# Position tables of a phasor stage made through PSUM, its first loads in another order, its last output tiles begun with two units open

## The reference, cut

```python
k_real = (x @ Wk).reshape(B, T, H, D)
v = (x @ Wv).reshape(B, T, H, D)
k = exp(1j * (k_real * 10.0))
rotors = exp(1j * (t[:, None, None] * freqs))
mem = cumsum(v * rotors);        out_pos = real(mem * conj(rotors)) / sqrt(t + 1)
ks = roll(k, 1), ks[0] = 0
mem = cumsum(v * conj(ks));      out_assoc = real(mem * k) / sqrt(t + 1)
out = out_pos * g_pos + out_assoc * g_assoc
y = out @ Wo
```

## Time and profile before

| | us |
|---|---|
| median of 3 runs | 3190.17 |
| lowest, highest | 3188.63, 3192.77 |
| the profiled execution | 3188.64 |
| its span | 3186.8 |
| mean granted TensorE clock | 0.961 of full speed |
| stage a, up to the first load of the next stage | 953.5 |

### The profile page before, as it was taken

The page is one execution under the profiler, slowest core; times in us unless marked ns, Lnnn a source line. Parts: engine busy times, 40 slices in busy tenths (PEclk is TensorE's granted clock), DMA queues, the critical chain, the costliest instruction groups (busy, mean ns, idle before and its releaser), DMA issues. The chain is left out here.

```text
span 3186.8 us, 38521 instructions
## 1 busy us (share of the span) xinstructions
PE 2836.8 (89%) x12161; PEld 1226.6 (38%) x12161; DVE 1842.2 (58%) x2419; ACT 2018.3 (63%) x2642; POOL 1304.6 (41%) x795
## 2 busy tenths in 40 slices
PE   1799999999988999655999999999999999969998
PEld 0355555555553444331323232323333332234443
DVE  7899999999974453454354444444534442044444
ACT  4554555455434555424979797888878888935554
POOL 7699898889872220051313132222213230021210
PEclk8899999999998999867999999999999999989999
DMA  2000011001003220205463553545462717231112
GB/s 79 0 30 27 23 39 33 26 20 39 20 24 110 67 66 29 88 14 109 51 133 54 103 85 78 92 85 93 72 115 47 126 27 146 27 113 42 64 53 66
DMA packets 164017, 200.46 MB, mean 63 GB/s; under 512 B 16504, under 2 KB 118272, under 8 KB 163840
## 3 DMA queue, kind: packets, MB, share of 16 engines
q1 hardware_dynamic: 163840, 198.25, 28.2%
HBM read 139.49 MB, written 58.72 MB: 62 GB/s over the span
## 5 line engine op out<-in xcount | busy, mean ns | idle before, releaser
L1819 ACT ACTIVATE b_pr<-b_ps 128x1024 f32<-128x1024 f32 x1024 | 1003.0, 1025 | 256.0 <-PE b_ps L1916 251.6
L1916 PE MATMUL b_ps<-b_st 128*128 128x512 bf16 x2048 | 591.8, 386 | 71.1 <-DMA b_st<-b_scratch 33.9
L1898 PE MATMUL b_acc<-b_pr,b_vaug 128*32 128x512 f32 x4096 | 548.6, 608 | 0.4 <-ACT b_pr L1819 0.4
L1916 PEld LDWEIGHTS b_ps<-b_st 128*128 128x128 bf16 x2048 | 150.5, 98 | 649.2 <-ACT b_pr L1819 380.3
L1217 PE MATMUL f_po<-f_s,f_w 128*128 128x512 f32 x768 | 352.0, 600 | 10.1 <-DVE f_xr L1002 6.3
L990 DVE TENSOR_TENSOR f_turned<-f_cs,f_s 128x1024 f32<-128x1024 f32 x96 | 119.4, 1244 | 364.7 <-ACT f_cs L1119 359.7
L604 PE MATMUL a_pv<-a_xnT,a_wv 128*128 128x512 f32 x512 | 249.9, 612 | 48.2 <-DVE a_mem L389 31.4
L596 PE MATMUL a_pu<-a_xnT,a_wk 128*128 128x512 f32 x512 | 237.4, 607 | 36.2 <-DVE a_frac L350 30.3
L1083 ACT ACTIVATE f_h<-f_po,f_b 128x512 f32<-128x512 f32 x192 | 131.9, 687 | 215.8 <-PE f_po L1217 215.8
L1535 POOL TENSOR_TENSOR b_SQ<-b_A 128x1024 f32<-128x1024 f32 x32 | 64.7, 2022 | 466.9 <-DVE b_A L1632 466.9
L643 PE MATMUL a_py<-a_wo,a_out 128*128 128x256 f32 x960 | 228.3, 381 | 0.0
(11 more groups left out here) (247 smaller groups left out, 4659.2 us busy)
## 6 DMA issues: line engine op xcount, KB each, us to landing
b_st<-b_scratch SPq DMA_DIRECT2D x512, 128.0 KB, 6.9
b_scratch<-b_parts SPq DMA_DIRECT2D x32, 768.0 KB, 8.2
f_xl<-x SPq DMA_DIRECT2D x16, 1024.0 KB, 5.5
f_xr<-x SPq DMA_DIRECT2D x16, 1024.0 KB, 6.8
a_xl<-in_L_attn_a_x_dram SPq DMA_DIRECT2D x16, 512.0 KB, 4.3
x<-a_xr SPq DMA_DIRECT2D x32, 256.0 KB, 2.2
x<-f_xr SPq DMA_DIRECT2D x8, 1024.0 KB, 4.5
b_xl<-x SPq DMA_DIRECT2D x8, 1024.0 KB, 7.7
```

The source lines that it names most:

```text
L1819: nc.scalar.activation(pr[:, 4 * (blk % 2) + j, :], ps[:, j % 2, :], ACT.Exp, scale=SC).then_inc(S["probs_done"], 1)
L1898: x = nc.tensor.matmul(acc[32 * j:32 * j + 32, h * 512:(h + 1) * 512], vaug[:, kt, c:c + 32], pr[:, 4 * (kt % 2) + j, h * 512:(h + 1) * 51 ...
L1916: x = nc.tensor.matmul(ps[:, j % 2, h * 512:(h + 1) * 512], st[:, g % 2, 1, j, kt * P:(kt + 1) * P], st[:, g % 2, 0, j, h * 512:(h + 1) * ...
```

## The change

The order of loads: x of batch 0 comes before wk, wk gets a semaphore of its own. The whole turns k of `reduce` and the second step of the wrap are kept in po, a PSUM tensor of stage a that nothing uses during the start, so that an operation of VectorE there has one tensor in SBUF. The first step of the wrap is made by ScalarE (`turns`, an Identity with scale and bias), the second and the addition by VectorE (`wrap`), the clamp by GpSimd. GpSimd makes all eight angles first, with the means between, and scales wk. The powers come later and read a tile of their own (tpos). `front(0)` stands after table 4 and `fraction(0)` after wrap(5). At the end four tiles are begun with c = 4 and 5 only, then four more, then c = 6 for all, then c = 7 for all; the last two additions of unit 63 are VectorE's.

```diff
@@ sync
                 sp.dma_start(freq_rows[:], ...).then_inc(freq_loaded, 16)
-                sp.dma_start(wk_sb[:], ...).then_inc(w_loaded, 16)
+                for h in range(2):
+                    sp.dma_start(xl[:, h * NJ:(h + 1) * NJ, :], xi[0, h]).then_inc(xl_loaded, 16)
+                sp.dma_start(wk_sb[:], ...).then_inc(wk_loaded, 16)
                 for a in range(HPT):
                     sp.dma_start(gates[...], ...).then_inc(w_loaded, 16)
-                for h in range(2):
-                    sp.dma_start(xl[:, h * NJ:(h + 1) * NJ, :], xi[0, h]).then_inc(xl_loaded, 16)
@@ gpsimd
-                post(NC * b + c, c, free)
+                post(NC * b + c, c, free, last and c == NC - 1)
-                def wrap(c):
-                    k = cos_t[:, c, :]
-                    pool.wait_ge(reduced, c + 1)
-                    nc.gpsimd.tensor_scalar(k, sin_t[:, c, :], 1.0 / TWO_PI, MAGIC, ALU.mult, ALU.add).then_inc(wrap_done, 1)
-                    pool.wait_ge(wrap_done, 2 * c + 1)
-                    nc.gpsimd.tensor_scalar(k, k, -MAGIC, -TWO_PI, ALU.add, ALU.mult).then_inc(wrap_done, 1)
+                def clamp(c):
+                    th = sin_t[:, c, :]
+                    pool.wait_ge(wrapped, c + 1)
+                    nc.gpsimd.tensor_scalar(th, th, PI_LOW, -PI_LOW, ALU.min, ALU.max).then_inc(clamped, 1)
-                for c in range(3):
+                for c in range(4):
                     angle(c)
+                means(0)
+                for c in range(4, NC):
+                    angle(c)
+                pool.wait_ge(wk_loaded, 16)
+                nc.gpsimd.tensor_scalar(wk_sb[:], wk_sb[:], TURN, 0.0, ALU.mult, ALU.add).then_inc(wk_scaled, 1)
+                scales(0)
+                for c in range(2):
+                    clamp(c)
                 ...
-                means(0)
-                for c in range(NC):
-                    wrap(c)
+                for c in range(2, NC):
+                    clamp(c)
                     if c == 3:
                         ...
-                    if c + 3 < NC:
-                        angle(c + 3)
-                    if c == 0:
-                        scales(0)
@@ vector
+                turns = po[:].rearrange("p a n -> p (a n)")
                 def reduce(c):
-                    th, k = sin_t[:, c, :], cos_t[:, c, :]
+                    th, k = sin_t[:, c, :], turns
                     dve.wait_ge(angle_done, c + 1)
+                    if c == 1:
+                        dve.wait_ge(reduced, 1)
+                    if c >= 2:
+                        dve.wait_ge(wrapped, c - 1)
                     ...
-                def clamp(c):
+                def wrap(c):
                     th = sin_t[:, c, :]
-                    dve.wait_ge(wrap_done, 2 * c + 2)
-                    nc.vector.tensor_tensor(th, th, cos_t[:, c, :], ALU.add).then_inc(wrapped, 1)
-                    dve.wait_ge(wrapped, c + 1)
-                    nc.vector.tensor_scalar(th, th, PI_LOW, -PI_LOW, ALU.min, ALU.max).then_inc(clamped, 1)
+                    dve.wait_ge(turns_done, c + 1)
+                    ...
+                    nc.vector.tensor_scalar(turns, cos_t[:, c, :], MAGIC, -TWO_PI, ALU.subtract, ALU.mult).then_inc(wrap_done, 1)
+                    dve.wait_ge(wrap_done, c + 1)
+                    nc.vector.tensor_tensor(th, th, turns, ALU.add).then_inc(wrapped, 1)
                 for c in range(NC):
                     reduce(c)
-                    if c == 1:
-                        dve.wait_ge(w_loaded, N_W)
-                        nc.vector.tensor_scalar(wk_sb[:], wk_sb[:], TURN, None, ALU.mult).then_inc(wk_scaled, 1)
                     if c >= 1:
-                        clamp(c - 1)
-                    if c == NC - 1:
+                        wrap(c - 1)
+                    if c == NC - 2:
                         fraction(0)
-                clamp(NC - 1)
+                wrap(NC - 1)
                 ...
                 batch(B - 1, last=True)
+                nc.vector.tensor_tensor(o, o, turn_c[:], ALU.add).then_inc(added, 1)
+                ...
+                nc.vector.tensor_tensor(o, o, turn_v[:], ALU.add).then_inc(unit_done, 1)
@@ scalar
+                def turns(c):
+                    act.wait_ge(reduced, c + 1)
+                    nc.scalar.activation(cos_t[:, c, :], sin_t[:, c, :], ACT.Identity, bias=cst[:, 0:1], scale=1.0 / TWO_PI).then_inc(turns_done, 1)
                 token_sums(0)
+                turns(0)
                 token_vars(0)
+                turns(1)
                 normalise(0, range(NT))
                 transposed(0)
                 for c in range(NC):
+                    if c + 2 < NC:
+                        turns(c + 2)
                     act.wait_ge(clamped, c + 1)
                     ...
-                    if c == NC - 3:
+                    if c == NC - 4:
                         front(0, 0, first=True)
@@ tensor
+                def begin(t):
+                    nc.tensor.matmul(tail[t], diag[:, t, :], xr[:, t, :], start=True, stop=False)
+                    for c in range(HC, NC - 2):
+                        nc.tensor.matmul(tail[t], out[:, c, t * P:(t + 1) * P], wo_sb[:, c, :], start=False, stop=False)
-                pe.wait_ge(unit_done, NC * B - 1)
+                pe.wait_ge(unit_done, NC * B - 2)
                 pe.wait_ge(xt_done, 4 * B)
                 pe.wait_ge(frac_done, NC * B)
                 pe.wait_ge(wo_done, 2 * NG * (B - 1) + NG)
+                for t in range(4):
+                    begin(t)
                 pe.wait_ge(odd_done, 2 * NC * B)
                 pe.wait_ge(even_done, 2 * NC * B)
-                for t in range(NT):
+                for t in range(4, NT):
                     if t == NT - 2:
                         pe.wait_ge(last_turned, NC * B)
-                    ...
+                    begin(t)
+                pe.wait_ge(unit_done, NC * B - 1)
+                for t in range(NT):
+                    nc.tensor.matmul(tail[t], out[:, NC - 2, ...], wo_sb[:, NC - 2, :], start=False, stop=False)
                 pe.wait_ge(unit_done, NC * B)
```

More of the change, by code:

```diff
@@ L93, in phase_a @@
         gates = s.sb("gates", [P, NC, 2])
-        sm = s.sb("sm", [P, 9, NT])
+        sm = s.sb("sm", [P, 10, NT])
         cst = s.sb("cst", [P, 4])
@@ L116, in phase_a @@
         w_loaded = s.sem("w_loaded")
+        wk_loaded = s.sem("wk_loaded")
         freq_loaded = s.sem("freq_loaded")
@@ L125, in phase_a @@
         reduced = s.sem("reduced")
+        turns_done = s.sem("turns_done")
         wrapped = s.sem("wrapped")
@@ L163, in phase_a @@
         xsum, vsum, ve, rstd, nmean = (sm[:, i, :] for i in range(5))
-        tcol, root, iroot, nmr = (sm[:, i, :] for i in range(5, 9))
-        N_W = 16 * (3 + HPT)
+        tcol, root, iroot, nmr, tpos = (sm[:, i, :] for i in range(5, 10))
+        N_W = 16 * (2 + HPT)
         N_SA = 3 * NC
@@ L186, in _ @@
                 sp.dma_start(freq_rows[:], freqs.rearrange("(c a) d -> c (a d)", a=HPT)).then_inc(freq_loaded, 16)
-                sp.dma_start(wk_sb[:], wk.rearrange("(k p) n -> p k n", p=P)).then_inc(w_loaded, 16)
+                for h in range(2):
+                    sp.dma_start(xl[:, h * NJ:(h + 1) * NJ, :], xi[0, h]).then_inc(xl_loaded, 16)
+                sp.dma_start(wk_sb[:], wk.rearrange("(k p) n -> p k n", p=P)).then_inc(wk_loaded, 16)
                 gv = gate.rearrange("(c a) g -> a c g", a=HPT)
@@ L261, in scales, with post @@
                     nc.gpsimd.tensor_tensor(nmr, nmean, rstd, ALU.mult).then_inc(rstd_done, 1)
-                def post(n, c, free):
+                def post(n, c, free, end=False):
                     s, o = c % 2, out[:, c, :]
@@ L275, in post @@
                     nc.gpsimd.tensor_tensor(halves(o), pair_of(s, 2), of_tokens(cos_k[:, s, :]), ALU.mult).then_inc(turned, 1)
+                    if end:
+                        return
                     pool.wait_ge(added, 2 * n + 1)
@@ L340, in _ @@
                 nc.vector.tensor_copy(turn_c[:], rnd[:].bitcast(I32)).then_inc(setup_v, 1)
-                nc.vector.tensor_copy(ve, tcol.bitcast(I32)).then_inc(setup_v, 1)
+                nc.vector.tensor_copy(tpos, tcol.bitcast(I32)).then_inc(setup_v, 1)
                 dve.wait_ge(freq_psum, 1)
@@ L362, in reduce @@
                     nc.vector.scalar_tensor_tensor(th, k, C2 / C1, th, ALU.mult, ALU.add).then_inc(reduced, 1)
-                def clamp(c):
+                def wrap(c):
                     th = sin_t[:, c, :]
-                    dve.wait_ge(wrap_done, 2 * c + 2)
-                    nc.vector.tensor_tensor(th, th, cos_t[:, c, :], ALU.add).then_inc(wrapped, 1)
-                    dve.wait_ge(wrapped, c + 1)
-                    nc.vector.tensor_scalar(th, th, PI_LOW, -PI_LOW, ALU.min, ALU.max).then_inc(clamped, 1)
+                    dve.wait_ge(turns_done, c + 1)
+                    if c + 1 < NC:
```

(41 more changed lines are left out.)

5 lines of the change are left out of this document (3 added, 2 removed).

## The result

The changed kernel took 3171.44 us (median of 5, 3165.83 to 3174.11) against 3189.89 for the kernel before: ratio 0.9941, 95% interval [0.993, 0.9953], 18.5 us less. The forecast was 3170.4 (3162 to 3178). One later run of the changed kernel took 3819.82 us at a mean granted TensorE clock of 0.727 and is in none of the times given here.

A forecast was written before the change was run, and what follows sets the result against it. VectorE was taken to bound the start of stage a and TensorE its end. Start 13.7 us plus end 6.1 gave 19.8 us off the median 3190.17: 3170.4 us, range 3162 to 3178.

The forecast's parts named there:

- Unit 0 at 69.0: Start of stage a: VectorE begins its first unit at 69.0 us instead of 81.07, 12.1 us earlier.
- the pitch: Start-to-start time of VectorE's table operations with PSUM: 1.255 us taken, between 1.22 and 1.32, six operations a table.
- The new wait before the first fraction: VectorE waits 2.8 us, since front(0) is behind turns(6) and table 4 on ScalarE.
- x and the scales: Start of stage a: sums start near 6.5 us instead of 18.74; GpSimd's scales end at 19.7 instead of 31.08.
- The slack at turns(2): ScalarE finishes turns(2) at 29.3 us, VectorE wants it at 29.9: 0.6 us to spare.
- GpSimd's first unit: GpSimd, which waits for all tables until 88.74 us, has them at 74.5; the first scan ends at 74.8.
- The end: TensorE's output tiles closing stage a start 3.5 us earlier, the clock stays at 1.00, finishing at 943.8: 6.1 us gained.
- The additions on VectorE: End of stage a: moving the last two additions from GpSimd to VectorE is worth nothing.
- What carries the start: VectorE's tables cost 7.5 us each, no less than 7.2; the gain is waits (15.7 us) and scaling (1.5) that go.
- the forecast's premise: Start of stage a: VectorE and GpSimd hold each other up in SBUF; VectorE's PSUM operands leave GpSimd free, 1.13 us per operation.
- The surcharge of a PSUM source: VectorE's table operations: the skill's 62 extra cycles per read, 2 us in all, would make 3172.4; the forecast took none.
- The rival of a fast tensor_scalar with PSUM: VectorE's table tensor_scalars run at twice the element rate, 0.76 us pitch: gain 27 us, 3163; chance 0.04.

The follow-up runs named there:

- the filled kernel: The kernel before with 13 identity matmuls into an unused PSUM tile, ahead of TensorE's wait for unit 62's output; 3195.55 us, ratio 1.0015.

## Why the prediction was right

The sum said 19.8 us in the profiled execution's terms; stage a gave 18.7, the span 17.2, the medians 18.5. That the median came within 1.1 us of the forecast, and stage a too, is in part luck. The kernel before came out 0.3 us lower than the median that the forecast started from. And the wait of VectorE at the odd product had its short value, 17.1 us, in both profiled executions: the second profile of the changed kernel has 18.7 there, and by it stage a is only 16.6 us shorter.

- *Unit 0 at 69.0*: it was 70.13. The term that was mis-sized is the pitch. I took 1.255 us from one row's gap of 0.04 us; the durations were right (1.22 to 1.23), but at two of the six operations, after the fourth and the sixth, the gap is 0.11, and the mean pitch is 7.70 / 6 = 1.283. Over 46 operations that is 1.3 us, more than the whole miss.
- *The new wait before the first fraction*, 2.8 us forecast: 2.70.
- *x and the scales*: sums at 6.44 (6.5), normalising at 18.79 (19.7), as GpSimd was even less held up than I allowed. The slack at turns(2) was 2.0 us and not 0.6.
- *GpSimd's first unit* at 74.8: 76.19, with unit 0; the 1.61 us before the second fraction went as forecast. Start in all 12.56 us (928.32 - 915.76, the last odd product) against 13.7.
- *The end*, 6.1 us: 6.14 (25.19 - 19.05). Its two parts are shown apart: 2.6 us of clock, in the filled kernel and in the tiles themselves (20.1 us of TensorE before, 17.5 after), and 3.5 us of earlier start (from 1.54 us behind the start of the last odd product to 1.98 ahead of it). The additions on VectorE were put at nothing, and are nothing.
- *What carries the start.* The prediction said that VectorE's own work would not shrink and that waits go. The runs agree (7.7 us a table against 7.2), and add what I did not separate. Taken one after the other, the 10.9 us at unit 0 are 2.9 for x first (81.07 to 78.21), 7.1 for the steps moved and the weights no longer waited for (to 71.11), and 1.0 for PSUM (to 70.13). The shares hang on the order: taken out of the changed kernel, x first costs 10.3. PSUM is worth so little since SBUF makes the tensor_scalars fast and the meeting with GpSimd slow, and since the one PSUM tensor brings waits of its own; with the wrap alone in SBUF, where GpSimd has little to do, the start is 3.0 us shorter still. So the forecast's premise, that GpSimd is only free because VectorE works on PSUM, held for the durations, but little of the gain rests on it.
- *The surcharge of a PSUM source.* By the Trainium skill, "VectorE: DVE Perf Modes", section on the TRN2 errata, it is an estimated 65 ns (62 cycles at the 0.96 GHz of that table). The traces do not agree: the tensor_scalar took 1.232 us from PSUM to PSUM (L369) and 1.227 from SBUF to PSUM (L382), and the addition took 1.220 with one operand in PSUM (L384) and 1.22 with both in SBUF where GpSimd left it alone (24.06 in the run with the wrap in SBUF).
- *The rival of a fast tensor_scalar with PSUM* did not come: L382 writes PSUM in 1.227 us, where the same operation in SBUF took 0.68. The Trainium skill, "VectorE: DVE Perf Modes", section on why PSUM operands drop a tier, excludes the fast one for fp32, and the traces agree.

## What to carry to other kernels

When two engines work on SBUF side by side, look at the same instruction beside different partners: the eight diagonal operations took 9.9 us beside VectorE's operations in SBUF and 2.8 beside those on PSUM, which told more than any busy share. In this kernel a PSUM operand freed the partner, at the price of 0.54 us for each tensor_scalar (1.23 against 0.69). So it pays where the partner has a queue that something waits for, and not where the partner has nothing to do. But first ask what the engine waits for. Here the steps moved between the engines were worth 7.1 us and PSUM 1.0, and with them went a wait of 11.3 us for all the weights that needed only one of them. An edit in an engine's order moves what is late next: price the next wait, here the fraction behind table 4, in the same sum.

## What the runs showed of the hardware, unexpected

- VectorE's start-to-start time was 1.26 us after a dependent operation of 1.22 to 1.23, and 1.33 to 1.34 where the next operation waits for two counters, the second of them that of the operation in front. With the wrap in SBUF the first reduction step still waits for two, but for none of the operation in front, and it starts 1.14 after the addition (24.06 to 25.20). Two waits alone thus cost nothing, and a dependence alone 0.12; the further 0.07 us show only where both come together.
- With 0.93 us of idleness before and 0.45 after the filling, TensorE's clock stayed at 1.00; after 2.15 us of idleness it had fallen to 0.50 though matmuls were then running (window 930 to 931 above). The length of the idle time alone does not tell which it will be: in the kernel before, 2.20 us of it in front of the product at 256.87 left the clock at 1.00 (window 257 to 258).
- The two gates transfers, 8 KB in all, took the queue for 9 us at 1 GB/s (6 to 15 us in the kernel before); x behind them moved at 312 GB/s and more.
- The same program's waits inside the units of stage a come out 2 us apart between executions, with equal starts.
